# Two-layer quantised FFN and routed expert FFN: the dense stage of one program ordered by batches of two steps

## What is computed

```python
x = x + _L0_ffn_ref(_L0_cond_ref(x, ...), ...)        # dense: silu(gate)*up, quantised, down
h = relu(x @ w1 + b1); y = x + h @ w2 + b2             # adapter
normed = (y - mean) * rsqrt(var + LN_EPS)
z = normed * gamma[lang] + beta[lang]
logits = z @ Wr; topk_w, topk_idx = top_k(softmax(logits), 2)
out = sum over experts e of cw[e] * (silu(z @ Wg[e]) * (z @ Wu[e])) @ Wd[e]
x = x + out
```

## Time and profile before

| what | us |
|---|---|
| median of 3 timed runs | 671.34 |
| lowest, highest | 667.01, 673.58 |
| the profiled execution, its device time | 666.66 |
| its span, first to last instruction | 664.9 |

### The profile page before, as it was taken

How to read it: one execution, slowest core, us unless ns; L and a number is a source line. 1 busy time by engine, 2 the same in 40 slices (tenths; PEclk the granted TensorE clock), 3 DMA queues, 4 the chain that set the end, 5 groups by cost and what they waited for, 6 DMA issues and landing times.

```text
span 664.9 us, 16051 instructions
## 1 busy us (share of the span) xinstructions
PE 604.4 (91%) x4404; PEld 412.9 (62%) x4404; DVE 510.1 (77%) x1373; ACT 442.2 (67%) x744; POOL 370.6 (56%) x573
## 2 busy tenths in 40 slices
PE   7988888898985558999999999999999999999994
PEld 2243335676663235777777777777777777777773
DVE  5589995688876879888988888888776666666652
ACT  3657995888864556888877787787665444445542
POOL 4014660047767683666657666667666555555544
PEclk9987999999998879999999999999999999999998
DMA  8524001256557649989899889866775556667552
GB/s 268 199 57 128 1 0 49 83 152 212 197 163 252 186 159 192 235 171 202 182 200 173 189 165 189 182 140 114 158 156 110 112 112 104 119 110 110 101 90 32
DMA packets 157300, 95.67 MB, mean 144 GB/s; under 512 B 107924, under 2 KB 150436, under 8 KB 157220
## 3 DMA queue, kind: packets, MB, share of 16 engines
q1 hardware_dynamic: 142900, 76.12, 47.7%
q0 software_dynamic: 13696, 18.51, 15.8%
q10 hardware_dynamic: 624, 0.03, 0.1%
HBM read 44.72 MB, written 24.68 MB: 104 GB/s over the span
## 4 chain that ended last, share of the span: by engine, by line
PE 55%; DVE 16%; issue 11%; POOL 6%; ACT 4%; DMA 3%; SPq 2%; another core or an unknown queue 1%; POOLq 1%; DVEq 0%; ACTq 0%
PE ps L692 29%; PE ps L743 15%; POOL rows L1643 3%; PE ps L564 2%; DVE big L1524 2%; PE ps L671 2%; DVE big L1364 2%; PE ps L803 1%; DMA small<-small 1%; DVE small L1189 1%; PE ps L582 1%; POOL small L1636 1%; PE ps L559 1%; DMA big<-in_low 1%
## 5 line engine op out<-in xcount | busy, mean ns | idle before, releaser
L692 PE MATMUL ps<-big,small 128*128 x1608 | 251.8, 313 | 2.8 <-ACT big L966 1.4
L692 PEld LDWEIGHTS ps<-big,small 128*128 128x128 f16 x1608 | 157.0, 98 | 81.3 <-issue 4.9
L1681 POOL DMA_INDIRECT out<-small x67 | 110.4, 1648 | 137.7 <-DVE small L1489 131.3
L743 PE MATMUL ps<-big,small 128*128 x1105 | 131.4, 273 | 0.5 <-DMA small<-small 0.5
L743 PEld LDWEIGHTS ps<-big,small 128*128 128x128 f16 x1105 | 105.3, 98 | 12.0 <-issue 0.6
L972 ACT ACTIVATE small<-small 128x704 f16<-128x704 f32 x67 | 52.6, 785 | 77.5 <-DVE small L1464 76.9
L1480 DVE SCALAR_TENSOR_TENSOR small<-small 128x64 f16<-128x64 f32 (+1 forms) x134 | 72.6, 583 | 19.9 <-ACT small L976 19.9
L1464 DVE SCALAR_TENSOR_TENSOR small<-ps,small 128x704 f32<-128x704 f32 x67 | 63.5, 948 | 24.9 <-PE ps L692 23.1
L976 ACT ACTIVATE small<-small 128x704 f16<-128x704 f32 x67 | 59.1, 882 | 28.0 <-DVE small L1474 28.0
L1643 POOL DMA_INDIRECT rows<-small x64 | 66.8, 1044 | 18.0 <-issue 18.0
L1654 POOL TENSOR_SCALAR small<-small 128x1 f32<-128x1 f32 x67 | 71.2, 1063 | 0.0
(11 more groups left out here) (256 smaller groups left out, 1048.7 us busy)
## 6 DMA issues: line engine op xcount, KB each, us to landing
small<-rows SPq DMA_DIRECT2D x67, 130.0 KB
big<-in_Wg SPq DMA_DIRECT2D x8, 704.0 KB, 4.6
big<-in_Wu SPq DMA_DIRECT2D x8, 704.0 KB
big<-in_Wd SPq DMA_DIRECT2D x8, 640.0 KB, 5.1
big<-in_xT SPq DMA_DIRECT2D x8, 512.0 KB, 7.1
small<-in_xT SPq DMA_DIRECT2D x16, 256.0 KB
out<-big SPq DMA_DIRECT2D x16, 256.0 KB
rows<-small SPq DMA_DIRECT2D x13, 130.0 KB, 4.2
```

What stands on the lines that cost most here:

```text
L692: m = e.matmul(ps[:, 2 * j + h, 0:352], xsT_(t)[:, 2 * xp + k, :], bigh[:, bass.ds(o + (4 * j + 2 * wp + k) * I + 352 * h, 352)], start=(n ...
L743: m = e.matmul(ps[:, 7, 0:H], hTE_(t)[:, hc_, :], bigh[:, bass.ds(o + 8 * I + (6 * wp + c) * H, H)], start=(n == 0), stop=(n == len(terms) ...
L1681: e.indirect_dma_start(out=out[:, :], out_offset=bass.IndirectOffsetOnAxis(ap=tok_(t), axis=0), in_=yw_(t), in_offset=None, compute_op=ALU ...
```

## The change

Every engine's loop over steps becomes a loop over batches. One `variance`, one `power` and one `logits` now serve both steps of a batch (four columns instead of two, twice), both `squares` stand together, both `gain`s (and with them both `adapter_out`s) stand together at the batch's end, and the `affine` of the even step moves behind the next batch's `variance`. `power` writes one of two buffers in turn. `keep_busy` drops from 4 a step and 3 a batch to 4 a batch (8 more once, in the last one); behind the loop it becomes 12, 6 and 10 matmuls around `piece_top`. `rank` of the last batch moves ahead of the first tile's `turn_rows`. The last batch's `affine`, `positions` and `payload` stand behind `x_lo(1)`. POOL scatters batch b-2 whole, behind `power(b)`; before, it scattered half of a batch behind each `power`. SP issues `load_l1` between `load_xk` and `store_x1`.

```diff
-            for i in range(1, 17):
-                if i == 2:
-                    dense_down(1)
-                if i >= 2:
-                    logits_and_rows(i - 2)
-                    adapter_in(i - 2)
-                if i <= ST and i != 2:
-                    dense_down(i - 1)
-                if i >= 2:
-                    adapter_out(i - 2)
-                if i >= 5 and i % 2 == 1:
-                    rank((i - 5) // 2)
...
+            for j in range(-1, NB):
+                step(dense_down, 2 * j + 1)
+                step(adapter_in, 2 * j)
+                step(logits_and_rows, 2 * j)
+                step(dense_down, 2 * j + 2)
+                if j == last:
+                    keep_busy(8, 0)
+                step(logits_and_rows, 2 * j + 1)
+                if j >= 0:
+                    keep_busy(4, 1)
+                step(adapter_in, 2 * j + 1)
+                step(adapter_out, 2 * j)
+                step(adapter_out, 2 * j + 1)
+                batch(rank, j - 1)
...
+            for j in range(-2, NB):
+                if j >= 0:
+                    step(floor_h, 2 * j + 2)
+                step(squares, 2 * j - 2)
+                step(squares, 2 * j - 1)
+                step(shift_h, 2 * j + 3)
+                if j >= 0:
+                    step(floor_h, 2 * j + 3)
+                step(shift_h, 2 * j + 4)
+                batch(second_weight, j - 1)
+                step(relu, 2 * j)
+                batch(adapter_gate, j)
+                batch(scale_beta, j)
+                step(evac_x1, 2 * j)
+                step(evac_x1, 2 * j + 1)
+                step(relu, 2 * j + 1)
...
+            for b in range(-2, last):
+                batch(payload, b - 1)
+                batch(variance, b)
+                step(affine, 2 * b - 2)
+                step(clip_h, 2 * b + 4)
+                if b == last - 1:
+                    order_experts()
+                batch(logits, b)
+                step(residual, 2 * b + 3)
+                if b == last - 1:
+                    first_tiles()
+                batch(route, b)
+                step(clip_h, 2 * b + 5)
+                step(affine, 2 * b + 1)
+                step(residual, 2 * b + 4)
+                step(gain, 2 * b + 2)
+                step(gain, 2 * b + 3)
+                batch(positions, b)
+            payload(last - 1)
+            variance(last)
+            affine(2 * last - 2)
             piece_scale(0)
...
             piece_lo(1, (0, 1))
             x_lo(1)
-            route(last)
-            piece_scale(2)
+            affine(ST - 1)
             positions(last)
             payload(last)
+            affine(ST - 2)
+            piece_scale(2)
...
-            for i in range(4, 18):
-                power(i - 4)
-                b, half = divmod(i - 7, 2)
-                if i >= 7:
-                    scatter(b, half)
...
+            power(0)
+            for b in range(1, NB + 2):
+                batch(power, b)
+                if b >= 2:
+                    scatter(b - 2, 0)
+                    scatter(b - 2, 1)
```

More of the change, by code:

```diff
@@ L156, in build_program @@
         vpe = carve(small, a, [2, 2])
-        rstd = carve(small, a, [2, 2])
+        rstd = [carve(small, a, [2, 2]) for _ in range(2)]
         pay_at = a[0]
@@ L271, in use, with step, batch @@
             return s // ring + 1
+        def step(of, s):
+            if 0 <= s < ST:
+                of(s)
+        def batch(of, b):
+            if 0 <= b < NB:
+                of(b)
         def hq_after(s):
@@ L503, in _ @@
                 e.dma_start(Xs[r:r + P, :], (padT, padB)[k % 2]).then_inc(S["pad"], 16)
-            for i in range(2, 17):
-                if i < ST:
-                    load_xk(i)
+            for i in range(2, ST):
+                load_xk(i)
+                if i >= 6 and i % 2 == 0:
+                    load_l1(i // 2)
                 store_x1(i - 2)
-                b = (i - 5) // 2 + 3
-                if i >= 5 and i % 2 == 1 and b < NB:
-                    load_l1(b)
             load_piece(0)
             load_piece(1)
+            store_x1(ST - 2)
             store_x1(ST - 1)
@@ L835, in _ @@
             piece_top(2)
-            rank(last)
             for t in range(TILES + 3):
@@ L1028, in _ @@
             e.activation(first_exp, pcol, ACT.Exp, scale=0.0)
[L1029 to L1042, removed]
-                if i >= 5 and i % 2 == 1:
-                    second_weight((i - 5) // 2)
+            for j in range(-2, NB):
[14 more added lines that the diff above has]
+                step(relu, 2 * j + 1)
             squares(ST - 2)
+            squares(ST - 1)
             piece_sum(0)
@@ L1048, in _ @@
             piece_hi(0)
-            squares(ST - 1)
             x_hi(0)
+            second_weight(last)
             piece_hi(1)
@@ L1053, in _ @@
             x_hi(1)
-            second_weight(last)
             piece_hi(2)
@@ L1536, in _ @@
             e.memset(hT1[64:65, :, :], 1.0).then_inc(S["one"], 1)
[L1538 to L1541, removed]
-                if i >= 2:
-                    residual(i - 2)
-                if i <= ST and i != 2:
-                    clip_h(i - 1)
-                if i >= 4:
-                    variance(i - 4)
-                if i >= 5 and odd:
-                    positions(rb)
-                if i == 16:
+            for b in range(-2, last):
[4 more added lines that the diff above has]
+                if b == last - 1:
                     order_experts()
+                batch(logits, b)
+                step(residual, 2 * b + 3)
+                if b == last - 1:
                     first_tiles()
-                if i >= 3:
-                    gain(i - 3)
-                if i >= 4:
-                    logits(i - 4)
-                    affine(i - 4)
-                if i >= 5:
-                    (payload if odd else route)(rb)
-            variance(ST - 2)
-            positions(6)
-            gain(ST - 1)
-            logits(ST - 2)
-            affine(ST - 2)
+                batch(route, b)
[8 more added lines that the diff above has]
+            affine(2 * last - 2)
             piece_scale(0)
-            payload(6)
-            variance(ST - 1)
+            logits(last)
+            route(last)
             piece_scale(1)
@@ L1719, in _ @@
                 products(n)
-            for i in range(4, 18):
-                power(i - 4)
-                b, half = divmod(i - 7, 2)
-                if i >= 7:
-                    scatter(b, half)
-            power(ST - 2)
-            scatter(5, 1)
-            power(ST - 1)
-            scatter(6, 0)
-            scatter(6, 1)
-            scatter(last, 0)
-            scatter(last, 1)
+            power(0)
[4 more added lines that the diff above has]
+                    scatter(b - 2, 1)
             side(0)
```

61 lines of the change are left out of this document (28 added, 33 removed).

## The result

| | before | changed |
|---|---|---|
| median, us | 670.82 | 694.53 |
| lowest, highest | 667.01, 673.58 | 692.73, 699.90 |
| profiled execution, its span | 666.66, 664.9 | 692.73, 691.0 |

The ratio is 1.0359, 95% interval 1.0307 to 1.0411: slower, where I had forecast 661.6. Tile 1's products, my measure, start at 259.07 instead of 234.87, so 24.2 of the 26.1 us between the spans arise before that point: 11.5 up to the last variance (220.89 to 232.41), 12.7 between it and tile 1 (14.0 to 26.7).

A forecast was written before the change was run, and what follows sets the result against it. No engine is full; a loop between engines bounds the stage at 6.15 us a step. Last variance 200.9 plus tail 24.3 puts tile 1 at 225.2, 9.7 earlier; off the median 671.34 that gives 661.6, range 653 to 670.

The forecast's parts named there:

- my measure: Start of tile 1's products on PE: forecast at 225.2, 9.7 us earlier than 234.87.
- First batch, its pace: Dense stage: first batch's variance at 120.6 to 120.9, then two batches at 10.8 us, before POOL sets the pace.
- POOL's pace of 11.27: POOL sets the pace from the third batch: 0.91 for the power plus eight scatters, 11.27 us against 11.90.
- my two ends: POOL's four-column power: extra cost between nothing and 0.72 over the two-column power's 0.72; 0 was taken.
- Rival 1: POOL and DVE hold each other up: power waits 0.6 a batch, pace 11.9, 666 in all; chance 0.15.
- The rule cited from the Trainium skill: Two-input DVE instruction and SBUF-reading POOL instruction contend; the later blocks fully, so POOL's power would wait for the affine's end.
- the 0.19 that I had taken: POOL's power beside DVE's affine costs 0.19 more, 1 us over five batches, from a scatter's 1.15 instead of 0.96.
- Last variance at 200.9: End of stage, batch 7: 120.9, two batches at 10.8, five at 11.27 give 198.9; with stalls 200.9.
- I expect stalls of the kind met inside the loop (3.3 us) again: DVE stalls the profile does not show: 3.3 us in the loop, some 1.3 absorbed by DVE's waiting.
- Rival 3: Language weights or x land late, pace stays 12.3, tile 1 at 232, gain 3 or less: 669; chance 0.12.
- Tail of 24.3: Last variance to tile 1's products: 24.3 to 24.5 us against 14.0, with batch 5's scatters behind the last power.
- Rival 2: PE with fewer fillers falls to its lower clock, losing 2.5 to 3 us a batch: 681; chance 0.07.

The follow-up runs named there:

- quiet chip: No program change: chips where the kernel before takes 656 to 660 and no trace has a remote wait in the stage; changed kernel there 658.17 beside 656.49.
- disturbed chip: No program change: chips where the kernel before takes 666 to 671 and traces have remote waits in the stage; changed kernel there 690.24, ratio 1.0303.
- e9: Changed kernel with each batch's eight scatters one batch sooner and all language loads early, on a disturbed chip: 673.71, ratio 1.0100.
- e8: Changed kernel with each batch's eight scatters one batch sooner, behind the next power, on a disturbed chip: 690.72, ratio 1.0356.
- fifth set: Runs e8 and e9 on one disturbed chip, beside the kernel before (666.43): 690.72 and 673.71.
- e1_break: Changed kernel with a spare two-column power between the two halves of each batch's eight scatters, on a quiet chip: 661.29 us.
- e1_again: Same edit as e1_break on the changed kernel, repeated on another quiet chip: 661.84.
- e1_timed: Same edit as e1_break on the changed kernel, timed on a further quiet chip: 663.49, ratio 1.0087.
- e10: e9's kernel with a spare power between the two halves of each batch's scatters, on a quiet chip: 656.33, ratio 0.9989.
- e3_again: Changed kernel with the old PE fillers put back beside its own, on a disturbed chip: 696.34, ratio 1.042.
- third chip: Quiet chip of the third set, where the changed kernel was run unaltered: 658.17 beside 656.49 for the kernel before, one run each.
- e7: Kernel before with the language loads of batches 3 to 7 issued before the first scatter, on a quiet chip: 656.94, ratio 0.9999.

## Why the prediction was wrong, step by step

- **First batch, its pace.** Variance at 120.6 to 120.9: it came at 119.80, about 1 early. Two batches at 10.8: 11.07 and 10.98. Right within 0.3.
- **POOL's pace of 11.27.** On a quiet chip it is 11.9 in three batches. From the power's start to the first scatter it takes 1.98 us where I had 0.91, and the eight scatters take 9.93 where I had 10.36. The power over four columns costs 1.21, not 0.72, between my two ends. In the batches of 11.9 it takes 1.38, 1.78 and 1.79. A trace parts two reasons: the power at 189.81 begins as far into an affine (0.46) as the one at 166.01, but without a clip behind it, and takes 1.35. So most of the 0.57 lost at 166.01 goes with the clip (0.55, L1216), and 0.14 is left for the affine, near the 0.19 that I had taken. Rival 1 has the pace of 11.9 right, but by luck in part: its wait of 0.6 was met in two batches, and a dearer power and cheaper scatters nearly cancel. The rule cited from the Trainium skill, "SBUF — State Buffer", "Who interferes with whom", is borne out only in that something is lost: the power at 202.44 begins 0.18 into an affine of 0.87 and takes the bare 1.21, so no full block is seen. On the disturbed chip it doesn't matter, since POOL waits there.
- **Last variance at 200.9.** On a quiet chip 202.06. That is near in part by luck: 2.0 of the 200.9 were for stalls, and a quiet chip has none. Without them I had 198.9, 3.2 too early: the five batches measure 59.7 us instead of 56.4.
- **"I expect stalls of the kind met inside the loop (3.3 us) again." This is the step that failed.** They sum to 50 us up to 225. The last variance came at 232.41, 30.3 behind the quiet chip's: five batches of 16.7 to 19.0 us instead of 11.0 to 12.9. I had read "remote" as chance events of DVE. The trace before told more: every waiter stood on a semaphore of PE whose matmul had ended 1.6 to 4.0 us earlier, and none of them came before the first scatter. The change lengthened the runs of scatters from four to eight. That language loads take part is shown by e9 against e8 (17.0 us), and that scatters do by where the waits begin and end (fifth set); that eight in a row instead of four turn 9 us of waits into 50 is what both traces look like, but the runs with a break (e1_break, e1_again, e1_timed, e10) all met quiet chips, so why the changed order suffers more stays open. Rival 3 had loads taking the pace, but by landing late; no engine waits for a DMA between 107 us and the last variance.
- **The gain was partly a loan.** I let the 8.9 us of stalls in the old kernel go but for 2. On a quiet chip the old order's last variance is at 211.75, 9.1 earlier than in the trace that I worked from, and the stage's real gain is 9.7 us, not 20.
- **Tail of 24.3.** 26.7 and on the quiet chip 27.0. The scatters of batch 5 end 13.7 behind the last variance (246.12) instead of 11.4, since two of them take 2.29 and 1.67 us instead of 0.96. The rows are issued 2.4 behind that end, as I had it. The rest (2.1 for `x_hi`, 8.4 to the products) is as worked out. On the quiet chip it is 13.4, 3.0, 2.3 and 8.4, again with two long scatters. Right in kind, about 2.5 too short, and the term is the run of scatters.
- **Rival 2, PE's clock.** The clock did fall (0.70), and matmuls took twice as long, but behind the waits: with the same list and no waits it stays at 1.00, and old fillers did not help (e3_again). A consequence, not the cause of the waits.

In sum: 9.7 us won in the stage and 11.6 lost in the tail make it nearly a tie where nothing disturbs it (658.17 against 656.49; with early loads 1.0019). In the main measurement the longer waits on PE's increments made it 3.6% slower.

## What to carry to other kernels

A wait on something the profile doesn't show is to be traced to its semaphore before it is called chance: if the instruction that increments it has ended, ask what traffic lies in between, and whether the change makes more of it in one stretch. Take the control along in every set of runs, on the chip of the experiment; three cures that all work are a warning. And what is moved in order to win in a loop (here POOL's scatters a batch later) is to be followed to the end of the loop, where it cost as much as the loop had won.

## What the hardware did that I had not expected

PE's semaphore increments can arrive late, with PE itself going on (164.83 to 172.40). In the waits read here they came 1.6 to 8.5 us behind the end of the matmul that carries them. It was seen on two of six chips and in the main measurement, only where POOL issues one indirect DMA behind the other, and only for PE.

The disturbed traces also hold fewer records of semaphore updates for the same program: 8,420 and 8,487 for the changed kernel, 10,117 on the quiet third chip, with the same 157,300 DMA packets. Nearly all that are missing are records of completed DMAs (5,599 and 5,670 against 7,148), and they are missing mostly between 140 and 280 us. The kernel before has as few, 8,605 (e7, its twin on a quiet chip, 10,150), though its waits are short: so the loss of records goes with the condition of the chip and not with the length of the waits. Whether increments and their records travel on one way that is overfull there, and whether recording is itself part of the delay, no run here could tell.
